# Latent attention: the second copy of each head's high query half, made by a transfer inside SBUF instead of a copy on VectorE

## The reference, cut to what matters

```python
q = einsum('bld,dhk->blhk', x, Wq)              # x after a layernorm; 16 heads of 64
latent = einsum('bld,dc->blc', x, Wkv_down)     # 64 numbers for each token
k = einsum('blc,chk->blhk', latent, Wk_up)
v = einsum('blc,chk->blhk', latent, Wv_up)
attn = einsum('bqhd,bkhd->bhqk', q, k) / sqrt(64)
attn = softmax(where(mask, attn, neg_inf))      # causal mask
y = einsum('bhqk,bkhd->bqhd', attn, v)
x = x + einsum('bqhd,hdo->bqo', y, Wout)
```

## Time and profile before

| | |
|---|---|
| Time, median of 3 runs | 2855.82 us (2855.44 to 2856.29) |
| The profiled execution | 2856.62 us, span 2854.4 us |
| Mean granted clock of the PE | 0.935 |
| PE busy | 2490.6 us (87%) |
| DVE busy | 2105.5 us (74%) |
| ACT busy | 1573.0 us (55%) |
| POOL busy | 877.8 us (31%) |
| Twins (line 2262) | first starts at 1807.6 us, last at 2593.3 us, 128 of them |

### The profile page before, as it was taken

How to read it: one execution, slowest core, us unless ns; L and a number is a source line. 1 busy time by engine, 2 the same in 40 slices (tenths; PEclk the granted TensorE clock), 3 DMA queues, 4 the chain that set the end, 5 groups by cost and what they waited for, 6 DMA issues and landing times. The chain is left out here.

```text
span 2854.4 us, 39741 instructions
## 1 busy us (share of the span) xinstructions
PE 2490.6 (87%) x14369; PEld 1354.2 (47%) x14369; DVE 2105.5 (74%) x3896; ACT 1573.0 (55%) x2523; POOL 877.8 (31%) x857
## 2 busy tenths in 40 slices
PE   7999999989999999999999777588888888898376
PEld 3444444444444444444444455255555555565254
DVE  3489688878879886888814455689779878877754
ACT  6655454545555554545554442277667767766251
POOL 4444343434443443444445500102112212202200
PEclk9999999999999999999999678699999999999677
DMA  5100000000000000000000100000000000000101
GB/s 181 54 1 1 0 1 1 1 1 1 1 1 1 1 1 1 1 1 1 1 1 1 49 16 0 1 2 2 2 3 2 2 2 2 2 2 1 49 16 59
DMA packets 29167, 33.09 MB, mean 12 GB/s; under 512 B 6404, under 2 KB 25396, under 8 KB 28964
## 3 DMA queue, kind: packets, MB, share of 16 engines
q1 hardware_dynamic: 27988, 27.88, 3.0%
q0 software_dynamic: 976, 2.56, 0.3%
HBM read 25.58 MB, written 4.19 MB: 10 GB/s over the span
## 5 line engine op out<-in xcount | busy, mean ns | idle before, releaser
L757 POOL TENSOR_TENSOR g_lo<-g_full,g_hi 128x512 f16<-128x512 f32 x512 | 670.5, 1313 | 900.6 <-ACT g_hi L849 899.0
L849 ACT ACTIVATE g_full<-hid,b_col 128x512 f32<-128x512 f32 x512 | 351.8, 687 | 562.2 <-PE hid L152 560.8
L150 PE MATMUL hid<-y_hi,w_hi 128*128 128x512 f16 x1024 | 396.9, 388 | 39.2 <-DVE y_lo L835 34.9
L151 PE MATMUL hid<-y_lo,w_hi 128*128 128x512 f16 x1024 | 396.0, 387 | 0.0
L152 PE MATMUL hid<-y_hi,w_lo 128*128 128x512 f16 x1024 | 395.3, 386 | 0.0
L150 PE MATMUL acc<-g_hi,w_hi 128*128 128x512 f16 x1024 | 389.5, 380 | 5.2 <-POOL g_lo L757 5.2
L151 PE MATMUL acc<-g_lo,w_hi 128*128 128x512 f16 x1024 | 389.4, 380 | 0.0
L152 PE MATMUL acc<-g_hi,w_lo 128*128 128x512 f16 x1024 | 389.2, 380 | 0.0
L849 ACT ACTIVATE g_hi<-hid,b_col 128x512 f16<-128x512 f32 x512 | 349.1, 682 | 0.0
L2139 DVE TENSOR_REDUCE mla_m_col<-mla_ps 128x1 f32<-128x512 f32 (+3 forms) x512 | 224.9, 482 | 62.2 <-PE mla_ps L1981 56.5
L2277 ACT ACTIVATE mla_p_full<-mla_ps 128x1280 f32<-128x1280 f32 x128 | 158.4, 1237 | 144.9 <-PE mla_ps L2011 144.6
(11 more groups left out here) (371 smaller groups left out, 4910.6 us busy)
## 6 DMA issues: line engine op xcount, KB each, us to landing
latent_stage<-in_L_ffn_w_dram SPq DMA_DIRECT2D x16, 512.0 KB, 4.7
x<-in_L_attn_x_dram SPq DMA_DIRECT2D x8, 512.0 KB, 8.5
routed_w<-in_L_ffn_w_dram SPq DMA_DIRECT2D x4, 1024.0 KB, 7.7
out_dram<-x SPq DMA_DIRECT2D x8, 512.0 KB, 4.8
mla_sums<-mla_sum_row SPq DMA_DIRECT2D x128, 2.0 KB
latent_stage<-in_L_attn_Wq_dram SPq DMA_DIRECT2D x1, 1024.0 KB, 8.5
latent_stage<-in_L_attn_Wout_dram SPq DMA_DIRECT2D x1, 1024.0 KB, 10.7
routed_wqkv<-in_L_ffn_wq_dram SPq DMA_DIRECT2D x2, 256.0 KB, 2.9
```

Of the source, the lines that this page charges most:

```text
L150: pe.matmul(out, w_hi, v_hi, start=first, stop=False)
L151: pe.matmul(out, w_hi, v_lo, start=False, stop=False)
L757: pool.tensor_tensor(g_lo[:, g, :], g_full[:, g, :], g_hi[:, g, :], ALU.subtract).then_inc(tail_done, 1)
L849: act.activation(out[:, g, :], hid[:, ht % 4, :], ACT.Gelu, bias=b1_col[:, ht:ht + 1], scale=1.0 / WS).then_inc(gelu_done, 1)
```

## The change

The DVE copy is gone. SP issues one DMA for each head instead, inside SBUF, from one half of `q_hi` to the other. The ACT now writes the second head of a pair straight to partitions 64 to 127, where its rows stand in PSUM too, and its twin goes to partitions 0 to 63. The one semaphore `q_twin` becomes four, by the head's parity and the pair's, each raised by 16 when a transfer has landed. The DVE's `q_lo` of the second head now waits for the ACT alone.

```diff
-        q_twin = sem("q_twin")
+        q_twin = [[sem(f"q_twin{i}{j}") for j in range(2)] for i in range(2)]
...
-                pe.wait_ge(q_twin, hn + 1)
+                pe.wait_ge(q_twin[hh % 2][hh // 2 % 2], 16 * (hb * (H // 4) + hh // 4 + 1))
...
                     dve.wait_ge(q_head, hn + i + 1)
-                    dve.tensor_copy(q_hi[LATENT:P, ring, :], q_hi[0:LATENT, ring, :]).then_inc(q_twin, 1)
-                    if i == 1:
-                        dve.wait_ge(q_twin, hn + i + 1)
                     dve.scalar_tensor_tensor(q_lo[0:LATENT, ring, :], ps[own, 6, :], 1.0 / WS, q_hi[own, ring, :],
...
                 for i in range(2):
-                    act.activation(q_hi[0:LATENT, (hh + i) % RING, :], ps[i * LATENT:(i + 1) * LATENT, 6, :], ACT.Copy,
+                    own = slice(i * LATENT, (i + 1) * LATENT)
+                    act.activation(q_hi[own, (hh + i) % RING, :], ps[own, 6, :], ACT.Copy,
                                    scale=1.0 / WS).then_inc(q_head, 1)
...
+            hb, hh, hn = head_of(b, h + LEAD)
+            if exists(hb) and h % 2 == 0:
+                for i in range(2):
+                    ring = (hh + i) % RING
+                    own, twin = (slice(j * LATENT, (j + 1) * LATENT) for j in (i, 1 - i))
+                    sp.wait_ge(q_head, hn + i + 1)
+                    sp.dma_start(q_hi[twin, ring, :], q_hi[own, ring, :]).then_inc(q_twin[i][hh // 2 % 2], 16)
```

## The result

| | before | after |
|---|---|---|
| Time, median of 4 runs each, one chip | 2856.06 us (2855.44 to 2856.61) | 2817.98 us (2817.49 to 2819.03) |
| Ratio, with its 95% interval | | 0.9867 [0.9850, 0.9884] |
| The profiled execution's span | 2854.4 us | 2816.0 us |
| PE, DVE, ACT busy | 2490.6, 2105.5, 1573.0 us | 2479.5, 2058.2, 1570.1 us |

The account below looks back on a forecast made before the run. Neither PE nor DVE alone bounds the kernel; their waits on each other decide. Pairs give 24.9 us, the clock 2, less 0.5 ahead of the loop: 26.4 off 2855.8, so 2829 us (forecast 2820 to 2840, range 2816 to 2852).

Parts of the forecast that it names:

- Steps 0 to 3: First steps of a 16-head batch: PE waits for the last maximum, so removing two twin copies gives 0.64 us per pair.
- Steps 4/5: Maxima could start 1.0 us earlier without twins, but y_lo needs the ACT's y_hi: 0.8 us a batch.
- Steps 6/7: y_hi runs without any wait before it, so 0.34 us at most, 0 in the other batch; taken as 0.17.
- Steps 8/9 and 14/15: 8/9: DVE in order throughout, 0.64 us; 14/15: DVE comes to wait for the PE's last tile, 0.13 us.
- The last batch: Four head pairs in the last batch, put at 2.7 us in all.
- q_lo in the GpSimd's time: q_lo, moved beside GpSimd work, keeps 0.68 us with one PSUM input; otherwise steps 4/5 give 0.5 instead of 0.8.
- The transfer: SP's twin DMA, taken at 2.7 us (1.9 to 3.5), hidden in the loop, costing 0.3 to 1.1 us once ahead.
- The clock: Falls of the PE's granted clock behind its waits: some may go, 0 to 6.6 us, taken as 2.
- The first batch and ahead of it: First batch's eight pairs give 2.4 us; of four pairs ahead three count, 1.7, less 0.5 for the transfer.
- C: Rival: more than counted, all four clock falls go and steps 6 and 14 give their 0.64: 2818 us; chance 0.08.
- B: Rival: cover given back by ACT or later p_lo, a fifth of the gain left: 2851 us; chance 0.14.
- A: Rival: rows through one or few DMA engines, twin usable after 5 to 5.8 us, +32: 2888 us; chance 0.10.

Follow-up runs that it names:

- experiment 1: Changed kernel with an unread DVE copy of the old size put back ahead of each q_lo, transfers kept: 2858.88 us, ratio 0.9999.
- experiment 4: Changed kernel with the unread DVE copy ahead of q_lo in steps 10 and 12 alone: 2821.53 us, ratio 0.9879.
- experiment 5: Changed kernel with the unread DVE copy ahead of q_lo in steps 0 and 2 alone: 2831.96 us, ratio 0.9914.
- experiment 2: Changed kernel without the 128 transfers, twin half zero, PE waiting for the ACT's q_hi alone: 2819.97 us, ratio 0.9872.
- experiment 6: Changed kernel with each head's transfer cut into two DMAs of 61 and 3 partitions, PE waiting for both: 2906.49 us, ratio 1.0175.

## Why the prediction was right, and where its sizes were not

**The bound.** Right. The time moved where the PE waited for the DVE's maxima and stood still where the DVE waited for the PE (steps 10 to 13; experiments 1, 4 and 5).

**Steps 0 to 3.** 0.64 each, as forecast, alike in all seven batches but for step 1 behind two turns of the loop.

**Steps 4/5: 0.80 forecast, 0.92 measured.** The term was bounded by y_lo waiting for y_hi. After, y_hi started while the exponential ahead of it still ran by its rows (2048.24 + 1.23 = 2049.47):

```profile
2048.24 1.23 ACT L2274 ACTIVATE mla_p_hi<-mla_ps 128x1280 f16<-128x1280 f32 x1
2049.36 0.60 ACT L2279 ACTIVATE mla_y_hi<-mla_ps 128x512 f16<-128x512 f32 x1
```

I had set it behind that end. This 0.11 is the missing 0.12.

**Steps 6/7: the term that was mis-sized most, 0.17 forecast, 0.59 and 0.71 to 0.75 with step 8.** I read y_hi as fixed in its place. After, y_lo does wait for it:

```profile
2062.14 0.69 DVE L2224 TENSOR_TENSOR mla_y_lo<-mla_ps,mla_y_hi 128x512 f16<-128x512 f32 x1 [0.67 <-ACT mla_y_hi L2279]
```

But the chain ahead of y_hi begins with the key scores of line 2007, and in the even batches these had waited up to 0.58 us for the maxima row, three times in the loop; that wait is gone there, also without the transfer (experiment 2). I had the row among the DMAs and did not use it here. In the odd batches y_hi does stay where it was, and step 7 gave 0.31, near the 0.34 that the forecast held possible. The other 0.28, in step 8, come from the p_lo behind it, shown here before and after (lines 2314 and 2312 are both o_lo):

```profile
1974.75 1.16 POOL L2314 TENSOR_TENSOR mla_o_lo<-mla_o,mla_o_hi 128x512 f16<-128x512 f32 x1 [4.75 <-ACT mla_o_hi L2286]
1974.86 2.39 DVE L2252 TENSOR_TENSOR mla_p_lo<-mla_p_full,mla_p_hi 128x1280 f16<-128x1280 f32 x1
```

```profile
1965.15 1.15 POOL L2312 TENSOR_TENSOR mla_o_lo<-mla_o,mla_o_hi 128x512 f16<-128x512 f32 x1 [4.22 <-ACT mla_o_hi L2283]
1965.53 2.12 DVE L2252 TENSOR_TENSOR mla_p_lo<-mla_p_full,mla_p_hi 128x1280 f16<-128x1280 f32 x1
```

The GpSimd's o_lo starts 0.38 us ahead of the p_lo instead of 0.11, lies beside it for 0.77 us instead of 1.05, and the p_lo is 0.27 shorter. This term alone is 0.5 a batch, 3 of the 5 us that the loop's batches gave over the forecast.

**Steps 8/9 and 14/15: 0.64 and 0.13 forecast, 0.76 and 0.25 measured.** In step 8 q_lo stands behind a p_lo and started 0.08 us before the p_lo's end (p_lo 2070.50 + 1.49, q_lo 2071.91), where the copy had started 0.04 after it. That is 0.12 more than the first copy's own 0.32. In experiment 1 copies put back cost 0.72 and 0.22 in these places. In step 10 0.07 is given back.

```profile
2070.50 1.49 DVE L2252 TENSOR_TENSOR mla_p_lo<-mla_p_full,mla_p_hi 128x1280 f16<-128x1280 f32 x1
2071.91 1.40 DVE L2262 SCALAR_TENSOR_TENSOR mla_q_lo<-mla_ps,mla_q_hi 64x512 f16<-64x512 f32 x2
```

In step 14 q_lo waits for the ACT, before and after, and that 0.12 has another cause. The PE's small query tile, which the forecast took as fixed, came behind the first maximum before (first block) and straight behind the value product after (second block):

```profile
2236.25 0.38 PE L2091 MATMUL mla_ps<-mla_p_hi,mla_val_hi 128*128 128x512 f16 x1
2237.24 1.68 DVE L2139 TENSOR_REDUCE mla_m_col<-mla_ps 128x1 f32<-128x512 f32 x4
```

```profile
2216.51 0.38 PE L2091 MATMUL mla_ps<-mla_p_hi,mla_val_hi 128*128 128x512 f16 x1
2218.14 0.27 PE L1980 MATMUL mla_ps<-mla_key_hl,mla_q_hi 128*128 128x256 f16 x1
2218.51 0.42 DVE L2139 TENSOR_REDUCE mla_m_col<-mla_ps 128x1 f32<-128x256 f32 x1 [0.30 <-PE mla_ps L1981]
```

From the product's start to the small tile it was 1.74 us before (to 2237.99) and is 1.63 now. These 0.11 come on top of the 0.13; the last maximum does wait for the PE's last tile now, as forecast.

**The last batch.** Its four pairs were put at 2.7 in all without a working; the terms of the steps give 2.25, and 3.4 were measured.

**q_lo in the GpSimd's time.** Right: its mean is 687 ns, 688 before, and none of the 128 is over 0.70 us, though 43 lie beside the GpSimd for more than 0.3 us. The rule of the Trainium skill cited for it ("SBUF — State Buffer", "Who interferes with whom") holds for q_lo here; of the 128 p_lo, 18 still take 2.1 to 2.3 us beside the GpSimd instead of 1.5.

**The transfer: hidden, as forecast, but for another size.** Taken at 2.7 us to use, it lands in 1.9 (median) and is used from 2.0 on (two in a row: mostly 4.0). The lower end of the range was the true value. By the fit of the Trainium skill cited with it ("DMA: Bandwidth & Descriptors"), which its section "Anatomy of one DMA — SWDGE (gpsimd) path" gives for DMAs of the GpSimd's software queue, the estimate was 2.15. SP's issues are 0.46 to 0.60 us in 120 of 128, and up to 1.67 in the rest, where 0.62 was taken. Ahead of the loop the sum took off 0.5. The trace has no wait for the transfer there: the two of the weight loads are in the first and the last batch, where experiment 2 gains nothing. So no run shows that term.

**The clock: 2 us forecast, 6.7 measured.** This is the other term that was mis-sized, and it is the upper end of its bounds: all four falls behind waits of the PE went. Experiments 1 and 5 bring falls back with the copies. The wait's length alone doesn't decide: before, six batches waited the same 1.73 us at step 1 and in only one of them the clock fell, and with two transfers in a row the PE waited up to 2.85 us there with no fall. What decides I leave open.

**The first batch and ahead of it.** 2.8 against 2.4: its pairs gave 0.64, 0.26, 0.21, 0, 0.77, 0.25, 0.64 and 0.25, where 0.56, 0.22, 0, 0, 0.64, 0.22, 0.56 and 0.22 were forecast, and 0.18 were given back at its start. Ahead of it 3.1 against 1.2: all four pairs won 0.64, not three 0.56, and the transfer cost nothing that shows. The other 0.57 lie in a step without a pair, where the granted clock over 11 us was 0.53 before (from 1829 us) and 0.69 after (from 1828).

**The rivals.** C, with a chance of 0.08, gave the very time, 2818, and was half right: the four falls did go and step 6 gave about its 0.64, but step 14 did not (0.25); the 0.12s above and the pairs ahead of the loop made up for it, so part of its fit is luck. B fell with the time itself, 2818 and not 2851: but for one step at a turn of the loop, no step of the loop's batches gave back more than 0.08. A did not happen because the rows are spread; where they are not (experiment 6), its mechanism and its use after "5 to 5.8" us are right (5.3), and its price of 32 us was too low: some 50 in the steps and up to 37 by the clock.

**What the views were to show.** The wait ahead of the large query tiles was to fall by about 20 us and fell by 9.4. In one step the 0.64 parted into a shorter stretch from the PE's value product to its small query tile (0.50: a wait of 0.34 for the first maximum was in it) and 0.13 of the large wait. The forecast took one wait where the DVE's delay stood in several. The distance between step 1 of two batches was to shrink by 3 us and shrank by 3.7 to 4.1 in the loop, and by 5.7 once, where a fall of the clock went too.

## What to carry to other kernels

To price an instruction taken off an engine, go step by step and ask who waits for that engine there; then follow every wait into the step, the small ones for a queue included, since they move too. One row's wait is a poor measure of the gain: measure the distance between two starts of the same instruction. A copy between partitions that nobody needs for some 2 us after its source is there belongs on a queue, if its rows are spread over many DMA engines; the same copy cut at 61 partitions lost more than the whole change had won.

## Hardware behaviour that I had not expected

- A transfer of 64 KB from 64 partitions of SBUF to 64 others lands 1.9 us after its issue starts (median of 128); the same 64 rows as 61 and 3 are usable after 5.2 to 5.3.
- Where a p_lo of the DVE and an o_lo of the GpSimd lay beside each other, the one that started second took longer. In the kernel before, the p_lo took 2.1 to 2.5 us in the 19 cases where o_lo had started first, and 1.5 in the 31 where the p_lo had, and there o_lo took 1.9 to 2.4 us instead of 1.2.
- Each DMA carried packets beyond its rows, 16 for 64 rows, 4 for 61 and 3 together.
- With the PE waiting for the transfer 45 times, up to 2.9 us, its mean granted clock over the layer was 0.95 instead of 1.00, as in this window of the changed kernel:

```profile
1845.00:2563.00 718.00, 646.57 (x5056) 421.46 (x5053) 589.21 (x970) 526.76 (x664) 133.05 (x202) 1.00 0.06 13
```

- The stalls at the turns of the loop differ from one execution to another: with nothing changed there, the first step of a turn came 1.1 and 2.0 us later in experiment 4 than in the changed kernel. Single differences of 2 us between two spans are not to be explained.
